# Second gate: output products in full width straight from the attention results

## What is computed

```
x = x + 0.5 * moe(layernorm(x))          # 8 experts, each row goes to its two best
x = x + attention(layernorm(x)) @ Wc     # 16 heads of 16, causal
x = x + 0.5 * moe(layernorm(x))
# moe: logits = h @ gate.T; weights of the two best, made to sum to one
#      a first choice that no row made is mapped to a similar expert
#      out = sum over the two of weight * down(silu(g(h)) * u(h))
```

## Time and profile before

| | us |
|---|---|
| median of 3 runs | 1220.74 (1218.36 to 1221.98) |
| the profiled execution | 1224.79 |
| its span, first to last instruction | 1223.0 |
| PE busy | 994.0 (81%) |
| PEld busy | 728.2 (60%) |
| DVE busy | 773.6 (63%) |
| ACT busy | 681.9 (56%) |
| POOL busy | 525.8 (43%) |

### The profile page before, as it was taken

One profiled execution on the slowest core, in us unless ns is written; L12 is line 12 of the kernel. 1 busy time (PEld: TensorE's weight loads), 2 busy tenths in 40 slices (PEclk: granted clock), 3 DMA queues, 4 the chain that ended last, 5 costly groups with the idle time before them and its releaser, 6 DMA issues. The chain is left out here.

```text
span 1223.0 us, 25340 instructions
## 1 busy us (share of the span) xinstructions
PE 994.0 (81%) x9110; PEld 728.2 (60%) x9110; DVE 773.6 (63%) x1560; ACT 681.9 (56%) x1601; POOL 525.8 (43%) x706
## 2 busy tenths in 40 slices
PE   5226999998789958999999999999865279999930
PEld 1125778777778845555555555555454268888830
DVE  3994444443468638888888888888229744444428
ACT  2723444444366513877787787877738545555420
POOL 1625667765546430223232232323342057777720
PEclk9667999999589975999999999999878689999975
DMA  9623555553547562336445454452256323333339
GB/s 305 235 80 99 201 188 196 192 184 128 176 133 242 176 159 52 95 98 144 101 118 116 109 123 109 100 108 69 55 154 244 130 76 102 104 104 103 102 131 316
DMA packets 100583, 172.96 MB, mean 141 GB/s; under 512 B 16240, under 2 KB 64368, under 8 KB 100464
## 3 DMA queue, kind: packets, MB, share of 16 engines
q1 hardware_dynamic: 86640, 133.57, 38.3%
q0 software_dynamic: 13824, 37.77, 9.1%
HBM read 101.55 MB, written 69.47 MB: 140 GB/s over the span
## 5 line engine op out<-in xcount | busy, mean ns | idle before, releaser
L1851 ACT ACTIVATE spare<-h_psS 128x512 f32<-128x512 f32 x576 | 306.6, 601 | 96.3 <-PE h_psS L1761 93.8
L1879 DVE TENSOR_REDUCE h_part<-h_psM 128x2 f32<-128x1024 f32 (+3 forms) x256 | 249.2, 1015 | 13.6 <-PE h_psM L1740 13.0
L1914 POOL TENSOR_SCALAR_AFFINE_SELECT spare<-spare 128x256 f32<-128x256 f32 x256 | 99.4, 406 | 307.2 <-ACT spare L1851 307.2
L919 PE MATMUL m_psG<-wgu,m_x_hi 128*128 x576 | 195.4, 421 | 1.2 <-DVE m_x_lo L993 1.2
L899 POOL DMA_INDIRECT ys<-m_y,m_slot_u x144 | 142.3, 988 | 79.9 <-ACT m_y L984 59.2
L1788 PE MATMUL h_psO<-spare,a_VP 128*17 128x256 f32 (+3 forms) x3072 | 167.9, 338 | 8.6 <-ACT spare L1842 8.4
L1740 PE MATMUL h_psM<-h_KT,h_QT 48*128 48x512 f32 (+3 forms) x768 | 145.1, 422 | 23.5 <-DMA h_QT<-a_QD 14.9
L1761 PE MATMUL h_psS<-h_QT,h_KT 49*128 49x512 f32 (+3 forms) x768 | 160.8, 409 | 4.1 <-ACT spare L1851 2.3
L893 POOL DMA_INDIRECT m_xg<-xn,m_slot_u x136 | 131.8, 969 | 51.0 <-PE m_psX L927 33.6
L1003 DVE TENSOR_TENSOR m_h<-m_act_g,m_psG 128x256 f32<-128x256 f32 x144 | 60.6, 421 | 136.6 <-ACT m_act_g L977 131.1
L919 PE MATMUL m_psY<-wdn,m_h_hi 128*128 x576 | 128.6, 305 | 11.1 <-issue 6.8
(11 more groups left out here) (234 smaller groups left out, 1627.1 us busy)
## 6 DMA issues: line engine op xcount, KB each, us to landing
xn<-spare SPq DMA_DIRECT2D x16, 512.0 KB, 3.0
wg_d<-wgu SPq DMA_DIRECT2D x16, 512.0 KB
p_yg<-ys SPq DMA_DIRECT2D x16, 512.0 KB, 5.4
a_KD<-spare SPq DMA_DIRECT2D x32, 256.0 KB, 3.0
h_KT<-a_KD SPq DMA_DIRECT2D x64, 128.0 KB
h_QT<-a_QD SPq DMA_DIRECT2D x64, 128.0 KB
a_OD<-spare SPq DMA_DIRECT2D x128, 64.0 KB, 2.4
wgu<-wg_d SPq DMA_DIRECT2D x16, 512.0 KB, 10.5
```

Of the source, the lines that this page charges most:

```text
L919: m = pe.matmul(out, s[:, c, :], ww[:, bass.ds(at + c * width, width)], start=(n == 0), stop=(n == 3 * CC - 1))
L1851: act.activation(prob[k % NP][:, h, :], psS[x % NS][:, :], ACT.Exp).then_inc(s_read, 1)
L1879: m = dve.tensor_reduce(out, psM[k % NM][:, :, at:at + n], AX.X, ALU.max, negate=True)
L1914: m = pool.affine_select(block, block, [[0, 2], [1, P]], ALU.is_ge, 0.0, 0, -1)
```

## The change

The second gate multiplies Y itself with w_c, both in plain fp32: two matmuls per tile where `three` made six. The high and low parts are made no longer, neither of Y (`high`, `low`) nor of w_c (in "project"); TensorE waits for GpSimd's `scaled` before groups 6 and 7, and SP for products where it waited for parts. VectorE's order is another: the first half's second choices come after add(4), the first low_places after the last add and the second choices, invert(1) and open_gap right after the choices. The first ranks come after group 6. Both one-hot tables lie in the lent area. Both gates end with a Silu of one column on ScalarE, and fill two of the four buffers of gathered rows; the experts' block issues the gathers of the other two first.

```diff
 def choices(self, dve, T, q, lg):
+self.choose(dve, T, q, 0, lg)
+self.second_choices(dve, T, q, lg)
+def second_choices(self, dve, T, q, lg):
 E, at, n = self.sh.E, self.tiles(q), self.size(q)
-self.choose(dve, T, q, 0, lg)
...
 at = room[0]
-part(4 * CC * HALF)
-y_hi, y_lo = ([lent.place(f"{name}_{n}{j}", [CC, HALF], at + (2 * i + j) * CC * HALF, F32R) for j in range(2)]
-              for i, n in enumerate(("y_hi", "y_lo")))
-own = Area(nc, ctx, f"{name}_own", NT * P // 2)
-oh_lo = [own.place(f"{name}_oh_lo0", [NT * P], 0, BF16), lent.place(f"{name}_oh_lo1", [NT * P], at, BF16)]
-den, rec = (own.place(f"{name}_{n}", [P], i * P) for i, n in enumerate(("den", "rec")))
+part(NT * P)
+oh_lo = [lent.place(f"{name}_oh_lo{i}", [NT * P], at + i * NT * P // 2, BF16) for i in range(2)]
+den, rec = sb("den", [Q, P]), sb("rec", [Q, P])
...
             gate_up(i)
-        sp.wait_ge(yhi_done, NG // 2)
-        sp.wait_ge(plo_done, CC * NG // 2)
+        sp.wait_ge(summed, NG)
...
             store(h)
-        sp.wait_ge(yhi_done, NG)
-        sp.wait_ge(dlo_done, NG - BY_POOL)
+        sp.wait_ge(summed, 2 * NG)
...
         for g in range(NG):
-            if g < BY_POOL:
-                pe.wait_ge(plo_done, CC * (g + 1))
-            else:
-                pe.wait_ge(dlo_done, g - BY_POOL + 1)
+            if g // 2 == LAST // 2:
+                pe.wait_ge(scaled_done, 2 * (g % 2) + 2)
...
                 for a in (2 * u, 2 * u + 1):
-                    y = [[s[g % 2][:, c, a * P:(a + 1) * P] for c in range(CC)] for s in (y_hi, y_lo)]
-                    w = [[w_c[s][:, c, :] for c in range(CC)] for s in range(2)]
-                    m = three(pe, psW[:, a, 0:CE], y[0], y[1], w)
+                    for c in range(CC):
+                        m = pe.matmul(psW[:, a, 0:CE], rows(g)[:, c, a * P:(a + 1) * P], w_c[:, c, :], start=c == 0,
+                                      stop=c == CC - 1)
                 m.then_inc(summed, 1)
-            if g == NG - 3:
+            if g == NG - 2:
...
     def _(act):
-        def high(g):
-            if g // 2 == LAST // 2:
-                act.wait_ge(scaled_done, 2 * (g % 2) + 2)
-            if g >= 2:
-                act.wait_ge(summed, 2 * (g - 1))
-            act.activation(y_hi[g % 2][:, :, :], rows(g), ACT.Copy).then_inc(yhi_done, 1)
...
-        for g in range(2):
-            high(g)
...
             square(g)
-            high(g + 2)
         deviate(0)
-        high(6)
         square(4)
-        normal(0)
-        high(7)
-        square(5)
-        normal(1)
-        square(6)
-        normal(2)
-        normal(3)
-        square(7)
+        for h in range(3):
+            normal(h)
+            square(5 + h)
         deviate(1)
-        for h in range(NG // 2, NG):
+        for h in range(3, NG):
...
             route.partitions(act, i)
+        act.activation(idle[:, :], consts["eps"][:, 0:1], ACT.Silu)
...
     def _(pool):
-        def low(g):
-            pool.wait_ge(yhi_done, g + 1)
-            for c in range(CC):
-                pool.tensor_tensor(y_lo[g % 2][:, c, :], rows(g)[:, c, :], y_hi[g % 2][:, c, :].bitcast(F32),
-                                   ALU.subtract).then_inc(plo_done, 1)
...
-        for g in range(4):
-            low(g)
...
                 scaled(q, z)
-        for g in range(4, BY_POOL):
-            low(g)
-        pool.wait_ge(plo_done, CC * BY_POOL)
...
         T_ = Seq(dve, route.dvs).then
-        def low(g):
-            dve.wait_ge(yhi_done, g + 1)
-            dve.tensor_tensor(y_lo[g % 2][:, :, :], rows(g), y_hi[g % 2][:, :, :].bitcast(F32), ALU.subtract
-                              ).then_inc(dlo_done, 1)
...
-        def choices(q):
-            dve.wait_ge(lg_done, NG * (q + 1))
-            route.choices(dve, T_, q, lg[:, route.tiles(q), 0:E])
+        def scores(q):
+            return lg[:, route.tiles(q), 0:E]
...
             add(g)
-        choices(0)
+        dve.wait_ge(lg_done, NG)
+        route.choose(dve, T_, 0, 0, scores(0))
         add(4)
+        route.second_choices(dve, T_, 0, scores(0))
+        add(5)
         invert(0)
-        add(5)
+        add(6)
         route.place(dve, T_, 0)
-        low(7)
-        add(6)
-        dve.wait_ge(rec_out, 16)
+        add(7)
+        dve.wait_ge(lg_done, 2 * NG)
+        route.choices(dve, T_, 1, scores(1))
+        invert(1)
+        route.open_gap(dve, T_, rstd[:, :])
         route.low_places(dve, 0)
-        add(7)
-        choices(1)
...
         route.shift(dve, T_)
-        invert(1)
-        route.open_gap(dve, T_, rstd[:, :])
...
             route.partitions(act, i)
+        act.activation(idle[:, :], consts["eps"][:, 0:1], ACT.Silu)
...
-R = 4
+R, FIRST = 4, 2
...
-gate(sem, slot_u, block_expert, xg, gathered)
+gate(sem, slot_u, block_expert, xg[0:FIRST], gathered)
...
             def gather(b):
-                pool.wait_ge(x_turned, b - R + 1)
+                if b >= R:
+                    pool.wait_ge(x_turned, b - R + 1)
...
+            for b in range(FIRST, R):
+                gather(b)
...
-self.w_c = [sb(f"w_c{k}", [P, sh.CC, sh.C + sh.M], F32R) for k in range(2)]
+self.w_c = sb("w_c", [P, sh.CC, sh.C + sh.M])
...
             m.then_inc(folded, 1)
-        pe.wait_ge(glo_done, 2)
+        pe.wait_ge(glo_done, 1)
+        pe.wait_ge(ghi_done, CC + 1)
...
         act.wait_ge(g_made, 1)
-        act.activation(w_c[0][:, :, C:C + M], psT[0][:, 0:CC * M].rearrange("p (c e) -> p c e", e=M), ACT.Copy
+        act.activation(w_c[:, :, C:C + M], psT[0][:, 0:CC * M].rearrange("p (c e) -> p c e", e=M), ACT.Copy
...
         deviate(2)
-        act.activation(w_c[0][:, :, 0:C], wc[:, :, :], ACT.Copy).then_inc(fhi_done, 1)
+        act.activation(w_c[:, :, 0:C], wc[:, :, :], ACT.Copy)
...
                           ALU.subtract).then_inc(glo_done, 1)
-        dve.wait_ge(ghi_done, CC + 1)
-        dve.tensor_tensor(w_c[1][:, :, C:C + M], psT[0][:, 0:CC * M].rearrange("p (c e) -> p c e", e=M),
-                          w_c[0][:, :, C:C + M].bitcast(F32), ALU.subtract).then_inc(glo_done, 1)
...
         combine(2)
-        dve.wait_ge(fhi_done, 3 * CC + 1)
-        dve.tensor_tensor(w_c[1][:, :, 0:C], wc[:, :, :], w_c[0][:, :, 0:C].bitcast(F32), ALU.subtract)
```

More of the change, by code:

```diff
@@ L305, in second_gate @@
     LAST = 2 * sh.B - 1
-    BY_POOL = NG - 1
     with ExitStack() as ctx:
@@ L326, in second_gate @@
         assert room[0] <= SPARE
-        lg = sb("lg", [P, NT, M])
+        lg, idle = sb("lg", [P, NT, M]), sb("idle", [P, 1])
         squares, std, rstd, shift = (sb(n, [P, NT]) for n in ("squares", "std", "rstd", "shift"))
@@ L333, in second_gate @@
         den_in, rec_done, rec_out, y_in, scaled_done = (sem(n) for n in ("den_in", "rec_done", "rec_out", "y_in", "scaled_done"))
-        yhi_done, plo_done, dlo_done, summed, x_done, lg_done = (
-            sem(n) for n in ("yhi_done", "plo_done", "dlo_done", "summed", "x_done", "lg_done"))
+        summed, x_done, lg_done = (sem(n) for n in ("summed", "x_done", "lg_done"))
         squared, std_done, rs_done, xn_done = (sem(n) for n in ("squared", "std_done", "rs_done", "xn_done"))
@@ L363, in _ @@
                     sp.wait_ge(o_out[r], 64 * (sh.B * H // 4))
-                sp.dma_start(den[0:Q, :], OD[heads_of, DH, :].rearrange("h (s t) -> h s t", t=P)).then_inc(den_in, 16)
+                sp.dma_start(den[:, :], OD[heads_of, DH, :].rearrange("h (s t) -> h s t", t=P)).then_inc(den_in, 16)
                 sp.dma_start(raw[:, :], OD[heads_of, 0:DH, :]).then_inc(y_in, 16)
@@ L367, in _ @@
                 sp.wait_ge(rec_done, 1)
-                sp.dma_start(RD[heads_of, :].rearrange("h (s t) -> h s t", t=P), rec[0:Q, :]).then_inc(rec_out, 16)
+                sp.dma_start(RD[heads_of, :].rearrange("h (s t) -> h s t", t=P), rec[:, :]).then_inc(rec_out, 16)
                 sp.wait_ge(rec_out, 16)
@@ L520, in invert @@
                     dve.wait_ge(rs_done, 2 * i + 2)
-                def choices(q):
-                    dve.wait_ge(lg_done, NG * (q + 1))
-                    route.choices(dve, T_, q, lg[:, route.tiles(q), 0:E])
+                def scores(q):
+                    return lg[:, route.tiles(q), 0:E]
                 route.prepare(dve, T_)
                 dve.wait_ge(den_in, 16)
-                dve.reciprocal(rec[0:Q, :], den[0:Q, :]).then_inc(rec_done, 1)
+                dve.reciprocal(rec[:, :], den[:, :]).then_inc(rec_done, 1)
                 for g in range(NG // 2):
                     add(g)
-                choices(0)
+                dve.wait_ge(lg_done, NG)
+                route.choose(dve, T_, 0, 0, scores(0))
                 add(4)
+                route.second_choices(dve, T_, 0, scores(0))
+                add(5)
                 invert(0)
-                add(5)
+                add(6)
                 route.place(dve, T_, 0)
-                low(7)
-                add(6)
-                dve.wait_ge(rec_out, 16)
+                add(7)
```

(4 more changed lines are left out.)

## The result

| | us |
|---|---|
| before, 4 runs | 1221.36 (1218.36 to 1224.18) |
| after, 4 runs | 1201.42 (1198.42 to 1204.14) |
| ratio | 0.9837, 95% interval 0.9803 to 0.987 |
| the profiled execution after | 1202.0, span 1200.3 |

What follows compares the result with a forecast made beforehand. TensorE's waits for high and low parts were taken to bound the second gate's first half, VectorE's dependent instructions the rest; 13.1 there plus 4.0 from moved gathers made 17.1, so 1220.74 would become 1203.6, range 1198 to 1213.

Steps and rivals of the forecast that it cites:

- The forecast case: Whole kernel: the gates save 17.1, so the median goes from 1220.74 to 1203.6; chance 0.82.
- Record: Second gate's new products: a full-width matmul's profile record takes 0.235 at full clock; sixteen half groups take 30.1.
- that rival: Second gate's products: weight loads of 0.108 don't hide under the columns, costing 13.8 more, 1217.4; chance 0.06.
- Clock: Start of the second gate's products: 4.5 at half speed before full clock, 2.3 lost, bounds 1.5 to 3.0.
- The low-clock rival: Second gate's products stay at 1.2 GHz as in the fold, so the kernel ends slower, 1230.5; chance 0.05.
- Stall and ranks: Second gate's products: TensorE waits 0.9 for group 5's add, and the first ranks behind the seventh group cost 0.6.
- GpSimd's scaled rows: Second gate, before group 6: rows ready by 916.5, group starts at about 920.7, so hidden with 4 to spare.
- VectorE's half and ScalarE: Second gate after the last add: ScalarE's first marked one-hot at 950.9, slot numbers 12.0 later at 962.9, 13.1 earlier.
- The cover of "as little as 0.4": Second gate: ScalarE is free at 948 to 950.5, before the first marked one-hot at 950.9; without cover at most 3.
- Handover: End of both gates: moving two gathers into the experts' block saves 2.0 each, 4.0 in all, bounds 0 to 5.0.
- Small parts: Project stage's two dropped subtractions save 0 to 1.2, taken as 0; the Silu at each gate's end 0.
- The tail's rival: Gates' ends: late ScalarE or fifth store (3), gathers (2) and handover (4) take 9 of 17, 1212.6; chance 0.07.

Runs made afterwards that it cites:

- e2: The kernel after with all four first gathers back in each gate; median 1274.2, ratio 0.9849 to the kernel before on the same chip.
- e3: The full-width products alone, with the kernel before's order of steps, four gathers and no Silu; median 1279.1, ratio 0.9897 to the kernel before.
- e7: The kernel after with the fifth store ahead of the second half of the output weights and three block places ahead of the second low places; 1200.9, ratio 0.9854.
- e8: e7 with the counts of the first second choices moved behind the add of group 5, and the first inversion behind them; 1198.8, ratio 0.9824.
- e6: The kernel after with the fifth store issued ahead of the second half of the output weights; 1200.1, ratio 0.9848 to the kernel before.
- e11: The kernel after without the Silu at the end of each gate; median 1268.7, ratio 0.983 to the kernel before on the same chip.
- e4: The kernel after with one of two matmuls per row tile left out, so results differ; median 1274.9, ratio 0.9855 to the kernel before.
- e10: e8 with the first inversion ahead of the first second choices and the first low places moved from VectorE to GpSimd; 1272.4, ratio 0.9851.
- e1: The kernel before, unchanged, run again on a slower chip; median 1291.7, ratio 0.9987.

## Why the prediction was right

The forecast case came in, 2.2 over the measured median. Step by step:

**Record.** At the full clock one half group follows the other by 1.80, so a record takes 0.225; 0.235 was put, bounds 0.222 to 0.247. Loads of weights are hidden, that rival is dead. Sixteen half groups are 28.8, 1.3 less than the 30.1 said. The "more work, 6.4" for TensorE was at the full clock on both sides; in busy time it was 1.9, since the old products ran in part at the low clock.

**Clock.** It was granted at 0.50 for the first four and 0.73 for the next four, and this cost 3.3 (the 96 records took 24.91, twelve half groups of 1.80 are 21.6) where I had 2.3, outside my bounds of 1.5 to 3.0. In e2, e3, e7 and e8 it cost 2.0. The low-clock rival did not occur: in all ten profiles with these products the granted clock is 1.00 from 8 to 20 behind their start, while the fold stood at 0.50 for 24. No run tells what makes that difference.

**Stall and ranks.** 0.92 (0.9 said), and 0.46 between the products around the ranks (0.6 said). With the adds the last one ends 34.7 after the start; 929.7 less 894.9 was 34.8. Two errors, in record and clock, cancelled each other.

**GpSimd's scaled rows.** Done at 908.3, 19.0 after the start, needed at 915.1: cover 6.8, more than the 4 said. But the compare of L175 ran beside them and took 0.53, where I had 0.29 both times: that small statement was wrong.

**VectorE's half and ScalarE.** The first marked one-hot is 21.5 behind the last add (21.2 said), the slot numbers 11.9 behind that (12.0 said): 13.1 earlier than before, as forecast. The cover of "as little as 0.4" was in truth missing by 0.45. The fifth store landed later than 2.9 after its issue would give, because that row was of a free queue. The same view of the second gate after, 885 to 970:

```profile
xn<-spare SPq DMA_DIRECT2D x8, 512.0 KB, 7.7
```

e6 puts the price of the fifth one's place at 0.2 to 0.6.

**Handover.** 2.5 in the first gate and 2.7 in the second, by e2; 2.0 each was said, bounds 0 to 2.5, 2.5 being what GpSimd's last gather alone would give, so the two are at and just over it. In the first gate GpSimd decides; in the second it may be VectorE now, as the prediction had left open. The price put beside it (at worst 1 per gate) was not paid: the third turn came 4.40 behind the first, as before. Another 0.5 in the second gate comes from GpSimd beginning its first gather 0.17 behind VectorE's slot numbers in place of 0.70 before; e2 and e3 show it too, so it isn't the gathers' number. Its cause stays open.

**Small parts.** 0 said for "project" and for the Silu; both are so: from the first gate's end to the heads it is 355.1 before and 355.3 after, and e11 shows it of the Silu.

Together the gates give 18.7 where 17.1 was said: 2.2 (the first gate's slot numbers came 0.4 later in the profile after, which takes from its 2.5) and 16.5. The rest of the difference of medians lies within what single runs vary; part of it may be the tail's clock. That the median came as near as 2.2 is in part luck: the two errors in the products cancelled, and the tail's clock was in no term. The tail's rival was wrong as a sum, but right in naming the place: of more time taken from TensorE's products nothing comes out (e4), as long as the stores hold ScalarE.

## What to carry to other kernels

Here plain fp32 took TensorE 1.80 per half group against 1.48 with the split parts, and needs no other engine, so where TensorE waits for the parts, the slower product is the faster one. After such a change halve the new suspected bound once: if the end stays, look at what the queue of transfers holds back, since a store issued behind weight loads sets when its buffer is free. What an engine must hand over at the end of a block (indirect gathers on GpSimd above all) is cheaper as the first work of the next block, as far as its consumer isn't there yet.

## What was not expected of the hardware

TensorE ran the same code, the tail of the heads, at either level of the clock from one profile to the next, 4.3 apart, and the clock's rise in the gate cost between 2.0 and 3.3; the two don't go together (e8: low tail, quick rise). GpSimd wrote a one-hot of 128 by 128 in 0.80 where VectorE needs 0.165 (e10). Two chips took 1292 to 1298 for the kernel before, the other 1220: in e1 the stages with the experts are 382.1 and 280.4 long where they were 355.1 and 238.7, and gate and heads are as before. No run tells why.
